# A vision tower on one core: the tail of the token stage in another order, and attentions with the key as the innermost dimension

## The chip, the cores and the metric

The kernel runs on one core of one Trainium2 chip. The metric is the device time of one execution in microseconds; lower is better. The kernel before has a median of 887.18 us over 3 runs (886.36 to 888.2).

## The reference

The input is 128 images x 3 channels x 128 x 128. Everything is float32. Cut to what matters here:

```
h = tok(x)                      # patches -> 9 window tokens + 1 class token per image: (128, 10, 256)
h = h + attn0(layernorm(h))     # 16 heads of 16 channels; scores (token 0, key 9) and (token 9, key 0) masked
h = h + moe(layernorm(h))       # 8 experts, top 2, GELU, layernorm per expert
h = h + attn1(layernorm(h))     # 16 heads; scores clipped to +-10 after scaling, causal
h = h + lora(layernorm(h))
```

An attention is: scores[t, s, head] = sum over 16 channels of q[t]*k[s]; weights = softmax over s; out[t] = sum over s of weights*v[s]; then a projection. The sequence is only 10 tokens long.

## The kernel before

The 128 images lie on the 128 partitions in all that follows the patches, so one tile is one of the 10 tokens, 128 x 256 (`h_at(t)`). The scores of an attention are no matrix product here: DVE (VectorE) or POOL (GpSimd) multiplies 256 channels of a query by 256 channels of n keys (`score_products`, L1121, or L1365 for the products on DVE, which read the query from PSUM), and a sum over 16 channels gives n x 16 scores (`add_up`, L1356). A "row" job is one query with all keys up to its own, a "column" job all earlier queries with one key. POOL's products go to slots in SBUF, two of them in turn; DVE adds them up (`pool_sums`). In attention 0 the columns of tokens 7, 8 and 9 are added up by PE (TensorE) with 16 matmuls each against the identity (`pe_sum_scores`, L1215), and ACT (ScalarE) copies the sums out (L1221).

Stages: (1) the token stage, 9 rounds over 9 patches, PE-bound; its tail (`pe_end`, `act_end`, `pool_end`, `dve_end`) is an order written out by hand for each engine in which the last two window tiles (agg, local and mod of tiles 7 and 8), the class token (`h_at(9)`, L1064) and the first part of attention 0 (turn_x, qk_tile, v_tile and the scores) are interleaved. Engines run their list in order and wait on semaphores. After it there is a barrier of all engines. (2) attention 0: masks, softmax in two halves of 5 tokens (`dve_attention`: L1403 maximum, L1404 subtraction, ACT's exponent L1332, L1408 sum, L1409 reciprocal, L1410 scaling), the value products (`value_products`, L1149: v times weight, the weight repeated over 16 channels) for even tokens on POOL and odd ones on DVE, each into one of two slots of its engine; the sum over keys is made by PE (L1275, 2 x 10 matmuls, 40 in the trace) or, for tokens 1, 3, 5 and 9, by DVE (L1418); PE turns the result (L300), projects it (L294), and `add_o` (L1437) adds it to h and takes statistics (L347, L349), with L354 and L341 (veps, nmr) and POOL's power (L336) at the end of a batch. A projection of token t waits for `add_o` of t-2. (3) the experts, PE-bound, with their weights streamed by DMA on SP's queue; the first weights are asked for when the scores of attention 0 are there. (4) attention 1, the same with n = t+1 keys, where masked scores come from a memset (L1383) and each row of scores is clipped in place (L1353). (5) a low-rank stage.

Scores and weights lie as token, key, head (`a_s`, `a_p`), heads innermost:

```
def score_place(kind, t, n):                                                  # L1143
    s4 = a_s[:, :].rearrange("p (t s h) -> p t s h", t=T, s=T)
    return s4[:, t, 0:n, :] if kind == "row" else s4[:, 0:n, t, :]
```

so the maximum and the sum over keys read with a step of 16 elements, and L1418 with a step of 256. All tensors in these stages are in SBUF but for the PSUM banks that PE writes.

Of the kernel before, what the change touches and what calls it, by code (L numbers as in the profile page):

```python
# [13 lines left out]
ALU = mybir.AluOpType  # L14
# [8 lines left out]
P = 128  # L23
# [40 lines left out]
def vision_tower(nc, d, out):  # L64
    ctx = ExitStack()
    with ctx:
# [861 lines left out]
        def pe_end(pe):  # L928
# [46 lines left out]
        def act_end(act):  # L975
# [109 lines left out]
        VALUES_ON_POOL = (0, 2, 4, 6, 8)  # L1085
        SUMS_ON_DVE = (1, 3, 5, 9)
# [15 lines left out]
        SUMS_ON_PE = {(T - 3, "column"): 0, (T - 2, "column"): 6, (T - 1, "column"): 7}  # L1102
# [12 lines left out]
        def of_query(x, t, n):  # L1115
            return x[:, t * T * H16:(t * T + n) * H16]

        def score_products(eng, kind, t, n, slot):
# [3 lines left out]
                                     a_qkv[:, t, second:second + C].unsqueeze(1).broadcast_to([P, n, C]), ALU.mult)  # L1122

# [30 lines left out]
        def half_scores(x, layer, g):

            nk = HALF if layer == 1 and g == 0 else T
            return x[:, :].rearrange("p (t s h) -> p t s h", t=T, s=T)[:, g * HALF:(g + 1) * HALF, 0:nk, :]


        VALUES_ON_DVE = [t for t in range(T) if t not in VALUES_ON_POOL]  # L1160

        def value_slot(t):
            if t in VALUES_ON_POOL:
                return a_prod[:, 2 + VALUES_ON_POOL.index(t) % 2, :]
            return a_prod[:, VALUES_ON_DVE.index(t) % 2, :]

        def wait_value_slot(eng, layer, t):

            mine = VALUES_ON_POOL if t in VALUES_ON_POOL else VALUES_ON_DVE
            i = mine.index(t)  # L1170
            if i >= 2:
                eng.wait_ge(sem("a_o_turned"), seen(layer, "o_turned", mine[i - 2] + 1))

        def pool_scores(pool, layer, first, last):

            jobs = pool_jobs(layer)
            for i, (t, kind, n) in enumerate(jobs):
                if first <= t < last:
                    pool.wait_ge(sem("a_qkv_made"), seen(layer, "qkv_made", 2 * t + 1))
                    if i >= 2 and summed_on_pe(layer, *jobs[i - 2][:2]):  # L1180
                        pool.wait_ge(sem("a_summed"), list(SUMS_ON_PE).index(jobs[i - 2][:2]) + 1)
                    elif i >= 2:
                        pool.wait_ge(sem("a_pool_prod_used"), used_count(layer, i - 2))
                    score_products(pool, kind, t, n, s_slot[1 + i % 2]).then_inc(sem("a_pool_prod_made"), 1)

        def pool_attention(pool, layer):
            if layer == 0:
                pool_route_constants(pool)
            else:
                inverse_std(pool, *batch_of("attention 1", 0))  # L1190
                inverse_std(pool, *batch_of("attention 1", 1))
                pool_scores(pool, layer, 0, 3)
                inverse_std(pool, *batch_of("attention 1", 2))
                pool_scores(pool, layer, 3, T)
            for t in VALUES_ON_POOL:
                pool.wait_ge(sem("a_p_made"), seen(layer, "p_made", 1 + t // HALF))
                wait_value_slot(pool, layer, t)
# [983 lines left out]
```

## Time and profile before

| | |
|---|---|
| median of 3 runs | 887.18 us |
| the profiled execution | 887.02 us, of which its span is 885.3 us |
| mean granted TensorE clock | 0.917 of full |
| PE, DVE, POOL, ACT busy | 85%, 62%, 45%, 40% of the span |
| tail of the token stage | to 442.4 us |
| attention 0, softmax and values | 442.5 to 512.2 us |
| attention 1, scores to the last projection | 774 to 852.2 us |

A row of the timeline or of the chain of waits begins with its start in microseconds from the span's start and its length. "x2" means that rows were merged. What stands in brackets is how long the engine was idle before it, and what released it. Names: PE matmul, PEld weight load, DVE VectorE, ACT ScalarE, POOL GpSimd. a_s are scores, a_p weights, a_prod value products, w_raw holds the slots of the score products.

### The profile page before, as it was taken

The numbers are of one execution on the slowest core, as the hardware profiler recorded it, in microseconds if no ns is written. First come the engines' busy times: TensorE is split into PE (matmuls) and PEld (weight loads), VectorE is DVE, ScalarE is ACT, GpSimd is POOL, SyncE is SP. The second block draws the span as 40 slices with busy tenths as digits, with TensorE's granted clock in tenths as the row PEclk, the third lists the DMA queues.
The fourth block names the chain that finished last, engine by engine and source line by source line (L and its number), as shares of the span: only waits on it lengthen the run. The fifth ranks groups of instructions, "written<-read, shape, count | busy, mean of one in ns | idle before, by whom it ended". The sixth has DMA issues, their size and how long they took to land.

```text
span 885.3 us, 13257 instructions
## 1 busy us (share of the span) xinstructions
PE 749.5 (85%) x4479; PEld 646.4 (73%) x4479; DVE 548.3 (62%) x1256; ACT 358.4 (40%) x897; POOL 396.1 (45%) x269
## 2 busy tenths in 40 slices
PE   2979999999999999984935964999999999580867
PEld 2869998898988986532835963999999998350756
DVE  1677877787777777667399643222222224799956
ACT  2465665665665655421000141444444443351131
POOL 4555757747757623575254302333333322144310
PEclk9899999999999999985968965999999998695899
DMA  8432132222221110000020038699998860400001
GB/s 269 143 123 80 47 91 77 79 82 83 83 83 42 39 58 1 1 0 0 1 96 1 25 129 324 245 325 325 339 326 332 322 241 19 147 1 0 1 1 60
DMA packets 34490, 102.77 MB, mean 116 GB/s; under 512 B 3624, under 2 KB 12152, under 8 KB 27000
## 3 DMA queue, kind: packets, MB, share of 16 engines
q1 hardware_dynamic: 31832, 94.84, 31.0%
q0 software_dynamic: 2592, 7.10, 2.1%
q8 instruction: 37, 0.61, 0.3%
q14 instruction: 29, 0.24, 0.1%
HBM read 95.75 MB, written 6.17 MB: 115 GB/s over the span
## 4 chain that ended last, share of the span: by engine, by line
PE 72%; DVE 19%; POOL 3%; DMA 2%; issue 1%; ACT 1%; SPq 1%; POOLq 0%; DVEq 0%; ACTq 0%
PE banks L1533 11%; PE banks L1541 11%; PE banks L287 9%; PE banks L289 9%; PE banks L288 9%; PE banks L294 6%; PE banks L1241 5%; PE banks L300 4%; DVE a_o L1418 3%; DVE a_prod L1149 3%; PE banks L1215 2%; DVE a_s L1356 2%; PE banks L1275 2%; PE banks L1871 1%; DVE w_raw L1365 1%
## 5 line engine op out<-in xcount | busy, mean ns | idle before, releaser
L401 POOL TENSOR_TENSOR x_lo<-xraw,x_hi 128x640 fp32r<-128x640 f32 x81 | 129.4, 1605 | 109.8 <-ACT x_hi L395 109.8
L287 PE MATMUL banks<-wc_hi,x_hi 128*128 128x256 f32 x405 | 121.8, 301 | 18.0 <-POOL x_lo L401 12.7
L1631 ACT ACTIVATE hid<-banks,b 128x128 f32<-128x128 f32 x216 | 79.3, 367 | 109.6 <-PE banks L1533 109.5
L288 PE MATMUL banks<-wc_lo,x_hi 128*128 128x256 f32 x405 | 116.4, 287 | 0.0
L289 PE MATMUL banks<-wc_hi,x_lo 128*128 128x256 f32 x405 | 116.4, 287 | 0.0
L287 PEld LDWEIGHTS banks<-wc_hi,x_hi 128*128 128x128 f32 x405 | 79.5, 196 | 20.5 <-issue 12.9
L1790 DVE TENSOR_TENSOR res<-banks,xb 128x256 f32<-128x256 f32 x27 | 11.5, 425 | 126.9 <-PE banks L1541 126.9
L288 PEld LDWEIGHTS banks<-wc_lo,x_hi 128*128 128x128 f32 x405 | 79.6, 196 | 1.8 <-issue 0.2
L289 PEld LDWEIGHTS banks<-wc_hi,x_lo 128*128 128x128 f32 x405 | 79.2, 195 | 0.0
L1275 PE MATMUL banks<-ident,a_prod 128*128 128x128 f32 x372 | 50.6, 301 | 32.7 <-POOL a_prod L1149 32.7
L424 DVE BATCH_NORM_STATS2 stats<-banks 128x6 f32<-128x256 f32 x81 | 34.6, 427 | 69.6 <-ACT pe_sb L418 68.9
L418 ACT ACTIVATE pe_sb<-banks 128x256 f32<-128x256 f32 x81 | 31.0, 383 | 111.8 <-PE banks L289 111.8
L1275 PEld LDWEIGHTS banks<-ident,a_prod 128*128 128x128 f32 x372 | 50.4, 218 | 34.4 <-POOL a_prod L1149 19.5
L287 PE MATMUL banks<-wkv_hi,xg_hi 128*128 128x512 f32 x162 | 70.9, 438 | 4.4 <-DVE xg_lo L485 4.2
L1533 PEld LDWEIGHTS banks<-xT,w_raw 128*128 128x128 f32 x448 | 67.5, 195 | 5.7 <-ACT xT L1619 0.9
L1533 PE MATMUL banks<-xT,w_raw 128*128 128x128 f32 x448 | 69.3, 279 | 0.5 <-ACT xT L1619 0.5
L1241 PE MATMUL banks<-a_w,a_xT 128*128 128x512 f32 (+1 forms) x160 | 65.9, 550 | 1.9 <-DVE w_raw L1365 1.8
L1669 POOL TENSOR_TENSOR y<-bve,mhalf 128x1 f32<-128x1 f32 x27 | 20.4, 755 | 104.6 <-DVE bve L1798 104.6
L1121 POOL TENSOR_TENSOR w_raw<-a_qkv 128x512 f32<-128x512 f32 (+9 forms) x15 | 47.2, 3151 | 44.6 <-ACT a_qkv L1312 20.7
L1541 PE MATMUL banks<-w_raw,hid 128*128 128x256 f32 x224 | 66.9, 380 | 0.0
L336 POOL TENSOR_TENSOR rstd<-veps,mhalf 128x5 f32<-128x5 f32 (+5 forms) x31 | 35.2, 1136 | 67.7 <-DVE veps L354 50.9
L1533 PEld LDWEIGHTS banks<-xT,w1more 128*128 128x128 f32 x416 | 61.8, 191 | 4.7
(293 smaller groups left out, 1830.0 us busy)
## 6 DMA issues: line engine op xcount, KB each, us to landing
w_raw<-in_w SPq DMA_DIRECT2D x28, 1024.0 KB
xraw<-in_x_main SPq DMA_DIRECT2D x27, 768.0 KB
w1more<-in_w SPq DMA_DIRECT2D x13, 1024.0 KB
w2more<-in_w SPq DMA_DIRECT2D x13, 1024.0 KB
xraw<-in_x_rest SPq DMA_DIRECT2D x27, 114.0 KB
yl<-y_rows SPq DMA_DIRECT2D x2, 1028.0 KB, 7.0
a_w<-in_qkv_w SPq DMA_DIRECT2D x2, 768.0 KB, 5.2
x_rows<-w_raw SPq DMA_DIRECT2D x5, 256.0 KB, 2.0
```

The source lines that it names most:

```text
L287: pe.matmul(dst, a[0], b[0], start=start, stop=False)
L288: pe.matmul(dst, a[0], b[1], start=False, stop=False)
L289: return pe.matmul(dst, a[1], b[0], start=False, stop=stop)
L294: last = pe.matmul(dst, aT[:, c * P:(c + 1) * P], w[:, c, a:b], start=(c == 0), stop=(c == CH - 1))
L300: last = pe.transpose(dst[:, c * P:(c + 1) * P], src[:, c * P:(c + 1) * P], ident[:, :])
L401: pool.tensor_tensor(x_lo[:, i % RING_X, :], xraw[:, k].rearrange("p c b -> p (c b)"), x_hi[:, i % RING_X, :], ALU.subtract).then_inc(sem( ...
L1121: return eng.tensor_tensor(slot[:, 0:n * C].rearrange("p (s c) -> p s c", s=n), a_qkv[:, 0:n, first:first + C], a_qkv[:, t, second:second ...
L1241: last = pe.matmul(dst, a_xT[:, t % 2, c * P:(c + 1) * P], a_w[layer][:, c, a:b], start=(layer == 1 and c == 0), stop=(c == CH - 1))
L1275: last = pe.matmul(bank(t % 2, c * P, (c + 1) * P), value_slot(t)[:, k * C + c * P:k * C + (c + 1) * P], ident[:, :], start=(k == 0), stop ...
L1533: last = pe.matmul(bank(fc % 2, 0, P), weights_of(s)[0][:, c * FF + fc * P:c * FF + (fc + 1) * P], xT[:, s % 2, c * P:(c + 1) * P], start= ...
L1541: last = pe.matmul(down_bank(s), hid[:, s % 2, fc, :], weights_of(s)[1][:, fc * C:(fc + 1) * C], start=(fc == 0), stop=(fc == FC - 1))
L1631: act.activation(hid[:, s % 2, fc, :], bank(fc % 2, 0, P), ACT.Gelu, bias=b1[:, bass.ds(e * FC + fc, 1)]).then_inc(sem("gelu_made"), 1)
```

## The change

The tail. On PE, ACT and DVE the steps agg, local and mod of tile 8 come one place earlier; DVE makes the scores of row 5 before it aggregates the class token, and sums column 5 behind that; POOL's power for the class token (`inverse_std` of batch 3) comes before the product of column 6 instead of behind it. POOL's score products get four places (two in `w_raw`, two in `a_prod`), and PE adds up columns 6 and 7 instead of 7, 8 and 9.

The attentions. Scores and weights lie as token, head, key. The maximum is no longer taken in attention 1; there DVE writes sums to PSUM, clips them from there to SBUF, and ACT takes the exponent row by row; the memset of the scores is replaced by one of the weights, on POOL. Half 0 of attention 1's softmax comes before row 9's sum. The reciprocal goes to PSUM. The weights of DVE's own tokens go to PSUM. DVE writes its value products with the key innermost (a step of n elements) and adds them up contiguously, now for all of its tokens. In attention 1 POOL takes tokens 0, 1, 2, 3, 4, 6, 8 and DVE 5, 7, 9.

```diff
 pe_end
+            turn_agg(pe, NW - 1)
             turn_x(pe, 0, 4)
             qk_tile(pe, 0, 3)
-            turn_agg(pe, NW - 1)
+            project_agg(pe, NW - 1)
             v_tile(pe, 0, 3)
-            project_agg(pe, NW - 1)
+            turn_local(pe, NW - 1)
             turn_x(pe, 0, 5)
+            project_mod(pe, NW - 1)
             qk_tile(pe, 0, 4)
-            turn_local(pe, NW - 1)
             v_tile(pe, 0, 4)
             turn_x(pe, 0, 6)
-            project_mod(pe, NW - 1)
...
 pool_end (job numbers now, tokens before)
-            pool_scores(pool, 0, 1, 3)
+            pool_scores(pool, 0, 0, 2)
             inverse_std(pool, *batch_of("attention 0", 1))
+            pool_scores(pool, 0, 2, 3)
+            local_std(pool, NW - 1)
             pool_scores(pool, 0, 3, 4)
-            local_std(pool, NW - 1)
-            pool_scores(pool, 0, 4, 5)
             inverse_std(pool, *batch_of("attention 0", 2))
             value_prod(pool, NW)
             fold_values(pool, NW)
-            pool_scores(pool, 0, 5, 7)
+            pool_scores(pool, 0, 4, 6)
             inverse_std(pool, *batch_of("attention 0", 3))
-            pool_scores(pool, 0, 7, T)
+            pool_scores(pool, 0, 6, T)
 dve_end
+            row_scores(dve, link, 0, 5)
             for half in range(2):
                 aggregate(dve, NW, half)
-            row_scores(dve, link, 0, 5)
+            pool_sums(dve, link, 0, 5)
             dve.wait_ge(sem("proj_done"), NW + 1)
...
             add_eps(dve, "attention 0", 3)
-            pool_sums(dve, link, 0, 5)
-            row_scores(dve, link, 0, 6)
+            shift_of(dve, *batch_of("attention 0", 3))
             pool_sums(dve, link, 0, 6)
-            shift_of(dve, *batch_of("attention 0", 3))
...
-        VALUES_ON_POOL = (0, 2, 4, 6, 8)
-        SUMS_ON_DVE = (1, 3, 5, 9)
+        POOL_VALUES = ((0, 2, 4, 6, 8), (0, 1, 2, 3, 4, 6, 8))
+        DVE_VALUES = tuple([t for t in range(T) if t not in pooled] for pooled in POOL_VALUES)
-        SUMS_ON_PE = {(T - 3, "column"): 0, (T - 2, "column"): 6, (T - 1, "column"): 7}
+        SUMS_ON_PE = {(T - 4, "column"): 0, (T - 3, "column"): 6}
+        def grid(x):
+            return x[:, :].rearrange("p (t h s) -> p t h s", t=T, s=T)
+        def weight_bank(g, a, b):
+            return bank(2 + g, a, b)
+        def scale_bank(g):
+            return bank(4, C + g * HALF * H16, C + (g + 1) * HALF * H16).rearrange("p (t h) -> p t h", t=HALF)
+        def job_place(layer, i):
+            return i % 2 if layer == 1 or i < 4 else (2, 3, 0, 1)[i % 4]
...
+        def row_exponent(act, t):
+            act.wait_ge(sem("a_p_cleared"), 1)
+            act.wait_ge(sem("a_s_made"), seen(1, "s_made", SCORED.index(t) + 1))
+            act.activation(grid(a_p)[:, t, :, 0:t + 1].rearrange("p h s -> p s h"), clipped(t), ACT.Exp, scale=D16 ** -0.5)\
+               .then_inc(sem("a_exp_made"), 1)
...
+                    if t >= 4:
+                        row_exponent(act, SCORED[t - 4])
...
+        SCORED = (0, 2, 1, 4, 3, 6, 5, 8, 7, 9)
         def clip(dve, link, layer, kind, t, n):
             if layer == 1:
-                st = score_place(kind, t, n)
-                link(dve.tensor_scalar(st, st, -40.0, 40.0, ALU.max, ALU.min))
+                dve.tensor_scalar(clipped(t), raw_scores(t, n), -40.0, 40.0, ALU.max, ALU.min)\
+                   .then_inc(sem("a_s_made"), 1)
...
+        def softmax_half(dve, link, layer, g):
...
+            link(dve.tensor_reduce(den_g, p_g, AX, ALU.add))
+            link(dve.reciprocal(scale_bank(g), den_g))
...
+            dve.tensor_tensor(share(p_g, pooled), share(p_g, pooled), scales(pooled), ALU.mult).then_inc(sem("a_p_made"), 1)
+            if mine:
+                dst = weight_bank(g, 0, len(mine) * T * H16).rearrange("p (t h s) -> p t h s", t=len(mine), s=T)
+                link(dve.tensor_tensor(dst, share(p_g, mine), scales(mine), ALU.mult))
...
+            for i, t in enumerate(DVE_VALUES[layer]):
+                n, slot = keys(layer, t), dve_slot(layer, t)
+                by_key = slot[:, 0:n * C].rearrange("p (h d s) -> p s h d", s=n, d=D16)
...
+                link(value_products(dve, layer, t, by_key))
+                dve.tensor_reduce(a_o[:, t * C:(t + 1) * C], slot[:, 0:n * C].rearrange("p (c s) -> p c s", s=n), AX, ALU.add)\
+                   .then_inc(sem("a_o_made"), 1)
                 while added < t - 3:
                     add_o(dve, layer, added)
                     added += 1
```

## Rows read from the trace of the kernel before

**Rows 1.** The page: span, and busy time, share and instructions by engine.
```profile
span 885.3 us, 13257 instructions
PE 749.5 (85%) x4479; PEld 646.4 (73%) x4479; DVE 548.3 (62%) x1256; ACT 358.4 (40%) x897; POOL 396.1 (45%) x269
```

**Rows 2.** The chain of waits, 400 to 442 us: start, length, engine, tile, line.
```profile
402.11 0.44 DVE h L1064
...
404.94 3.43 POOL w_raw L1121
...
410.25 2.57 DVE nmr L341
...
421.06 20.95 PE banks L1215 x96
```

**Rows 3.** The timeline of the same tail.
```profile
393.31 0.76 PE L1239 MATMUL banks<-bias_r,pick 64*128 64x512 f32 x1 [3.65 <-DVE w_raw L1365]
...
408.83 8.47 POOL L1121 TENSOR_TENSOR w_raw<-a_qkv 128x1792 f32<-128x1792 f32 x2
...
412.74 2.27 DVE L1365 TENSOR_TENSOR w_raw<-a_qkv,banks 128x2048 f32<-128x2048 f32 x1
```

**Rows 4.** Groups on DVE, 300 to 560 us: busy us, mean ns; idle before.
```profile
L1418 DVE TENSOR_REDUCE a_o<-a_prod 128x256 f32<-128x2560 f32 x4 | 18.3, 4564 | 0.1
...
L1408 DVE TENSOR_REDUCE a_den<-a_p 128x80 f32<-128x800 f32 x2 | 3.0, 1492 | 0.0
...
L1365 DVE TENSOR_TENSOR w_raw<-a_qkv,banks 128x2560 f32<-128x2560 f32 x1 | 2.8, 2821 | 0.0
L1356 DVE TENSOR_REDUCE a_s<-w_raw 128x160 f32<-128x2560 f32 x1 | 2.8, 2819 | 0.0
...
L1356 DVE TENSOR_REDUCE a_s<-w_raw 128x48 f32<-128x768 f32 x2 | 1.9, 949 | 0.0
```

**Rows 5.** The timeline of attention 0's softmax and values.
```profile
450.86 9.81 POOL L1149 TENSOR_TENSOR a_prod<-a_qkv,a_p 128x2560 f32<-128x2560 f32 x2 [6.77 <-DVE a_p L1410]
...
452.91 3.35 DVE L1410 TENSOR_TENSOR a_p<-a_p,a_rden 128x800 f32<-128x800 f32 x1
...
455.56 7.42 PE L1275 MATMUL banks<-ident,a_prod 128*128 128x128 f32 x40 [13.57 <-POOL a_prod L1149]
456.30 7.06 DVE L1149 TENSOR_TENSOR a_prod<-a_qkv,a_p 128x2560 f32<-128x2560 f32 x1
...
467.84 2.81 DVE L1149 TENSOR_TENSOR a_prod<-a_qkv,a_p 128x2560 f32<-128x2560 f32 x1
...
493.33 2.69 DVE L354 TENSOR_SCALAR veps<-mv 128x4 f32<-128x4 f32 x1
...
498.40 4.63 PE L1275 MATMUL banks<-ident,a_prod 128*128 128x128 f32 x40
...
510.34 1.89 PE L294 MATMUL banks<-a_wo,a_oT 128*128 128x256 f32 x8
```

**Rows 6.** The timeline of attention 1.
```profile
774.31 1.39 DVE L1383 MEMSET a_s<- 128x1600 f32 x1 [0.28 <-ACT a_qkv L1312]
...
781.09 0.60 ACT L1312 ACTIVATE a_qkv<-banks 128x512 f32<-128x512 f32 x1 [0.80 <-PE banks L1241]
...
784.84 3.23 DVE L1353 TENSOR_SCALAR a_s<-a_s 128x80 f32<-128x80 f32 x1
...
794.88 0.60 ACT L1312 ACTIVATE a_qkv<-banks 128x512 f32<-128x512 f32 x1 [1.33 <-PE banks L1241]
...
796.14 1.28 ACT L1332 ACT_TABLE_LOAD   x1
...
819.44 0.69 DVE L1149 TENSOR_TENSOR a_prod<-a_qkv,a_p 128x512 f32<-128x512 f32 x1
...
850.35 1.89 PE L294 MATMUL banks<-a_wo,a_oT 128*128 128x256 f32 x8
```

**Rows 7.** Busy us by engine in tile 0's stretch, PEclk granted clock, DMA share, GB/s.
```profile
455.50:463.00 7.50, 7.42 (x40) 7.26 (x40) 7.47 (x2) 0.00 (x0) 5.17 (x1) 0.62 0.00 0
```

More of the change, by code:

```diff
@@ L1154, in half_scores @@
[L1154 to L1172, printed above, removed]
+            s4 = grid(a_s)
@@ new lines, in score_place, with key_weights @@
+            return (s4[:, t, :, 0:n] if kind == "row" else s4[:, 0:n, :, t]).rearrange(
+                "p h s -> p s h" if kind == "row" else "p s h -> p s h")
+        def key_weights(layer, t, n):
+            if t in DVE_VALUES[layer]:
+                i = [q for q in DVE_VALUES[layer] if q // HALF == t // HALF].index(t)
+                p_t = weight_bank(t // HALF, i * T * H16, (i + 1) * T * H16)
+            else:
+                p_t = a_p[:, t * T * H16:(t + 1) * T * H16]
+            return p_t.rearrange("p (h s) -> p s h", s=T)[:, 0:n, :].unsqueeze(3).broadcast_to([P, n, H16, D16])
@@ new lines, in half_scores, with pool_slot, dve_slot, job_slot @@
+        def half_scores(x, layer, g, first=0, step=1):
+            return grid(x)[:, g * HALF + first:(g + 1) * HALF:step, :, 0:half_keys(layer, g)]
+        def pool_slot(layer, t):
+            return a_prod[:, 2 + POOL_VALUES[layer].index(t) % 2, :]
+        def dve_slot(layer, t):
+            return a_prod[:, DVE_VALUES[layer].index(t) % 2, :]
+        def job_place(layer, i):
+            return i % 2 if layer == 1 or i < 4 else (2, 3, 0, 1)[i % 4]
+        def job_slot(layer, i):
+            k = job_place(layer, i)
+            return s_slot[1 + k] if k < 2 else a_prod[:, k - 2, :]
@@ L1174, in pool_scores @@
         def pool_scores(pool, layer, first, last):
             jobs = pool_jobs(layer)
[L1177 to L1184, printed above, removed]
+            for i in range(first, last):
+                t, kind, n = jobs[i]
+                pool.wait_ge(sem("a_qkv_made"), seen(layer, "qkv_made", 2 * t + 1))
+                earlier_use = [j for j in range(i) if job_place(layer, j) == job_place(layer, i)]
+                if earlier_use:
+                    pool.wait_ge(sem("a_pool_prod_used"), used_count(layer, earlier_use[-1]))
+                score_products(pool, kind, t, n, job_slot(layer, i)).then_inc(sem("a_pool_prod_made"), 1)
@@ L1328, in act_attention @@
                         copy_qkv(act, 1, t - 1)
+                    if t >= 4:
+                        row_exponent(act, SCORED[t - 4])
                 copy_qkv(act, 1, T - 1)
-            for g in range(2):
-                act.wait_ge(sem("a_s_made"), seen(layer, "s_made", g + 1))
-                act.activation(half_scores(a_p, layer, g), half_scores(a_s, layer, g), ACT.Exp, scale=D16 ** -0.5)\
-                   .then_inc(sem("a_exp_made"), 1)
+                for t in SCORED[T - 4:]:
+                    row_exponent(act, t)
+            else:
+                for g in range(2):
+                    act.wait_ge(sem("a_s_made"), g + 1)
+                    act.activation(half_scores(a_p, 0, g), half_scores(a_s, 0, g), ACT.Exp, scale=D16 ** -0.5)\
+                       .then_inc(sem("a_exp_made"), 1)
             for t in range(T):
@@ L1367, in row_scores @@
             dve.wait_ge(sem("a_query_used"), len(rows_on_dve(0)) * layer + rows_on_dve(layer).index(t) + 1)
-            link(add_up(dve, "row", t, n, s_slot[0]))
+            link(add_up(dve, layer, "row", t, n, s_slot[0]))
             clip(dve, link, layer, "row", t, n)
@@ L1395, in half @@
-            def half(x, g):
-                return x[:, g * HALF * H16:(g + 1) * HALF * H16].rearrange("p (t h) -> p t h", t=HALF)
-            def over_s(x, g, nk):
-                return half(x, g).unsqueeze(2).broadcast_to([P, HALF, nk, H16])
-            for g in range(2):
-                s_g = half_scores(a_s, layer, g)
-                link(dve.tensor_reduce(half(a_max, g), s_g.rearrange("p t s h -> p t h s"), AX, ALU.max))
-                dve.tensor_tensor(s_g, s_g, over_s(a_max, g, s_g.shape[2]), ALU.subtract).then_inc(sem("a_s_made"), 1)
@@ L1405, in dve_attention @@
-            for g in range(2):
-                p_g = half_scores(a_p, layer, g)
-                dve.wait_ge(sem("a_exp_made"), seen(layer, "exp_made", g + 1))
-                link(dve.tensor_reduce(half(a_den, g), p_g.rearrange("p t s h -> p t h s"), AX, ALU.add))
-                link(dve.reciprocal(half(a_rden, g), half(a_den, g)))
-                dve.tensor_tensor(p_g, p_g, over_s(a_rden, g, p_g.shape[2]), ALU.mult).then_inc(sem("a_p_made"), 1)
-            dve.wait_ge(sem("a_p_made"), seen(layer, "p_made", 2))
@@ L1412, in dve_attention @@
-            added = 0
-            for t in VALUES_ON_DVE:
-                wait_value_slot(dve, layer, t)
-                ins = value_products(dve, layer, t, value_slot(t))
-                if t in SUMS_ON_DVE:
-                    link(ins)
-                    dve.tensor_reduce(a_o[:, t * C:(t + 1) * C],
-                                      value_slot(t)[:, 0:keys(layer, t) * C].rearrange("p (s c) -> p c s", c=C), AX, ALU.add)\
-                       .then_inc(sem("a_o_made"), 1)
-                else:
-                    ins.then_inc(sem("a_dve_values_made"), 1)
+                link(dve.memset(grid(a_s)[:, 0, :, T - 1], NEG4))
@@ new lines, in dve_attention @@
+                link(dve.memset(grid(a_s)[:, T - 1, :, 0], NEG4))
+                for g in range(2):
+                    s_g = half_scores(a_s, 0, g)
+                    max_g = a_max[:, g * HALF * H16:(g + 1) * HALF * H16].rearrange("p (t h) -> p t h", t=HALF)
+                    link(dve.tensor_reduce(max_g, s_g, AX, ALU.max))
+                    dve.tensor_tensor(s_g, s_g, max_g.unsqueeze(3).broadcast_to([P, HALF, H16, T]), ALU.subtract)\
+                       .then_inc(sem("a_s_made"), 1)
```

84 lines of the change are left out of this document (49 added, 35 removed).

## The prediction

> **What bounds the kernel now.** I read the page first: the span and the busy line [rows 1] show PE at 85% on average, but the slices show two thin places for it, around 390 to 530 us and 750 to 850 us. These are the places that the change touches, so the average says nothing here. Then I read the chain of waits, stage by stage, and the timeline under it.
>
> Stage A, the tail of the token stage (up to 442.5 us). The chain goes through the last tile's residual h(9) at 402.11, two POOL products, a stretched nmr on DVE, the tile's projection and then 21 us of PE adding columns 7, 8 and 9 [rows 2]. The reader is to see that PE works alone at the end, and that the way there is queueing: PE stood 3.65 us for DVE's product of row 5 [rows 3] and then ran tile 8 at about half pace.
>
> Stage B, the softmax and values of attention 0 (442.5 to 512.2), is DVE's: one-source reductions whose inner step is large, and instructions with two SBUF inputs that stand behind POOL [rows 4, 5]. Stage C, attention 1 (774 to 852.2), is DVE's as well [rows 6]. The expert stage between B and C and the LoRA stage behind C are not touched; they start as much earlier as what is before them ends.
>
> **DVE's prices.** A reduction of 768 inner-contiguous elements takes 0.949 us, one of 2560 takes 2.819 [rows 4], so a contiguous one costs 0.15 + 1.04 per 1000 elements. With the key as outer dimension 800 elements took 1.492 and 2560 took 4.564 [rows 4]: 0.67 ns an element more. A product of 2560 with one operand in PSUM takes 2.82 [rows 4], one from SBUF alone 2.81 when POOL is idle [rows 5].
>
> **A.** Removed: column sums 8 and 9 leave PE for DVE; column 6 goes from DVE to PE. Moved: agg(8), local(8) and mod(8) on PE, ACT and DVE; DVE's row 5 ahead of aggregate(9); inverse_std(3) on POOL ahead of column 6; POOL has four slots and no longer waits for PE's sums. No DMA moves.
> 1. h(9). Row 5's product no longer stands behind aggregate(9), so PE's wait of 3.65 goes [rows 3]. PE is then not idle, so tile 8, at half clock from 393.3 to 400, runs partly at full clock; of the 3.4 this can give I take 1.85, since mod(8) may stall PE a little. aggregate(9) ends near 391.5 as before, ahead of PE's arrival. h(9): 402.1 - 5.5 = 396.6; its statistics end 1.3 later, 397.9.
> 2. POOL is idle by then (row 6's product ends at 396), so inverse_std is done at 398.5. But its next instruction, column 6's product, is free to start at once, and nmr (two SBUF inputs) comes 0.1 later. Before, nmr took 2.57 beside a POOL product instead of 0.15, ending with it [rows 2, 3]. I expect the same: nmr ends with column 6's 3.43, at 402.0.
> 3. From 402.0 DVE has, back to back: row 6's sum (1792) 2.0, row 7 two of 2048 4.6, row 8 two of 2304 5.1, column 8's sum 2.3, row 9 two of 2560 5.7, column 9's sum 2.55: 22.3 with gaps 22.5, so 424.5. POOL: columns 7, 8, 9 are ready at 406, 410.5 and 415.6 (8.47 for 1792 + 2048 [rows 3]), before DVE wants each. PE: from nmr's end to its first sum 8.2 us as before (412.8 to 421.1 [rows 2]), 410.2; columns 6 and 7 by the old rate, 20.95/24 = 0.873 per key [rows 2], 13 keys 11.3, 421.5 and a copy, 421.9. DVE ends last. Against 442.4: **-17.9**.
>
> **B**, counted from the first memset. Softmax: four reductions of 800 fall from 1.49 to 0.98 (-2.0). The scaling of half 1 took 3.35 instead of 0.99, until POOL's product ended [rows 5]; now it has one SBUF input: -2.36. Splitting each scaling in two adds 0.15 each, +0.3. So p_made(0) comes at 6.5 instead of 8.3, and DVE is free at 9.9 instead of 13.8. Products: the first took 7.06 for 2.81, behind POOL [rows 5]; now 2.82. Sums 4.56 become 2.82, and tile 7, which PE summed with 40 matmuls, gets one on DVE (+2.82), with PE's 4.63 [rows 5] gone. So 5.7 for each of five tiles: 15.6, 21.3, 27.0, and with two adds (1.05 each: add, statistics, their merge) before each, 34.7 and 43.5; add_eps after tile 3 still stands behind POOL (2.69 for 0.17 [rows 5]), which is in the last number with about 1.
> PE becomes the bound: tile 0 from 11.3 (POOL 4.64) at the low clock, 7.4 [rows 5], 18.7; tile 1 and a projection 20.8; tile 2 25.5; projections with tile 3 and add_o(0) 28.4; tile 4 33.0; projections and tile 5, after add_o(2), 36.1; tile 6 40.8, projection and tile 7 42.2; projection 6 waits for add_o(4) at 43.9, 45.1; tile 8 49.8; the end, as before, 3.2 later: 53.0. Before it was 512.2 - 442.4 = 69.8 [rows 5]. **-16.8**.
> What I price by bounds: the product now writes with a step of 40 bytes. No row has DVE writing so. [...] Above: what a large step costs on reading, +1.71 for 2560 (4.56 against 2.82). [...] POOL reads the weights with the same step: 4.64 to 5.60 (its full-stream product has 2.2 ns an element by the 8.47 above); I take 4.64, since only every 16th element moves on; the upper end costs 1.0, once, at tile 0. Reciprocals that write to PSUM: 0 to 0.1 each.
>
> **C.** The memset of 1.39 goes [rows 6] (POOL's of a_p, about 1.5, falls into 5 us in which POOL waits for the combine). Row 0 moves from 775.7 to 774.05, and PE, which waited for it, with it: a tile's copies come every 2.8, row 9's at 793.2 instead of 794.88 [rows 6]. Clips stood behind POOL (3.23 for 0.2 [rows 6], and 1.59 and 1.09); they now read PSUM. DVE: rows 0, 2, 1 until 778.2, wait for tile 4 780.1, rows 4 and 3 until 784.8, wait 785.6, rows 6, 5 until 791.9, row 8 797.4, row 7 800.0, softmax of half 0 (400 elements: 0.57, 0.65, 0.57) 801.9, row 9 2.82 + 0.3, 805.0, its exponent on ACT 0.5, softmax of half 1 (0.98, 0.65, 0.49, 0.65 and gaps) 808.4. Maxima and subtractions (0.83, 0.58, 1.48, 0.99) are gone, as is the 3.2 of the last scaling. Values start at 808.4, not 819.44 [rows 6]. ACT's exponents, 0.2 to 0.4 each, lie in the 1.0 that ACT idles per tile; the table load of 1.28 [rows 6] now comes at tile 4, where xT is made one tile ahead of its use; without that cover it costs 1.28.
> Values: DVE keeps tiles 5, 7, 9: 3.6, 4.6, 5.7 with two adds between them: 812.0, 818.7, 826.9 (one add waits 1 for PE). PE has tiles 0 to 4 from 802.8, at the low clock at first, and is at tile 6's end by 824.8. Then as before: add 4, projection 6 828.4, tile 8 4.2, 832.6, and 3.0: 835.6 against 852.2 [rows 6]: **-16.6**.
>
> Sum: 887.02 of the profiled execution (its span 885.3 and 1.7 around it) - 17.9 - 16.8 - 16.6 = 835.7. The median is 0.2 above that execution: **836**.
>
> [...] The trace has DVE reductions with a large step 1.6 times as dear as contiguous ones [rows 4]. [...]
> The product with a PSUM operand took 2.82, the one without 2.81 [rows 4, 5]. [...]
>
> **Rivals.**
> 1. Writes with a step cost what reads do. B: 7.35 per tile on DVE, add_o(4) at 51.4, end 60.2, +7.2; C: 0.67 ns on 6144 elements, +3.9. 836 + 11 = 847. For it: one memory. [...] 0.22.
> 2. Slower than before: the same place, but a step on writing costs far more. Rival 1 has 11.1 us for 0.67 ns, 16.6 us per ns; from 3.1 ns an element (a product of 2560 at 10.7 us, 3.8 times itself) the whole 51 is gone, at 4 ns the time is 902. Nothing in the rows has such a factor. 0.02.
> 3. nmr gets in ahead of POOL: A ends 3.4 earlier, 832. For it: in the trace nmr was issued 1.4 after POOL had begun, so the order is untried. Against: POOL's next instruction follows 0.0 us after the last. 0.12.
> 4. PE keeps the low clock through B. It was granted 0.62 in tile 0 with PE full [rows 7], tile 8's 4.63 are full clock [rows 5]. Five tiles at 7.3, ten projections at 1.9 and five turns at 0.6 are 59 from 11.3: 70, B gains nothing, 853. Against: in the stretch where it works without gaps it got the high clock. 0.05.
> 5. The weights in PSUM do not free DVE: a product still stands behind POOL's. Then the first two or three of B wait 2 to 4 each, C's 2: +10, 846. Against: the product of 2048 with the query in PSUM took 2.27, its own price, beside POOL's products [rows 3]. 0.05. That the edits do nothing of what they say has 0.01.
> The forecast itself, 831 to 841, has 0.53.
>
> **How the numbers follow.** The range takes in the forecast, rival 3 and rivals 1 and 5 with a few us for my step-by-step errors in A (h(9) between 395 and 402 moves the end by 5): 829 to 850. Within 0.2% (1.8 us, about what a measurement can tell from no change) I put 0.01, slower 0.02, faster 0.97.
>
> **What would show it.** A: the h(9) addition near 397, nmr stretched to some 3.4, PE's sums over before DVE's last sum near 424. B: DVE products of 2560 at 2.8, sums at 2.8, none behind POOL; PE busy from 11 us on and waiting only for add_o. C: clips at 0.2 throughout, values from 808 less what A and B gave. Wrong if products take 4.5, if PE's clock stays low, or if h(9) does not move.

## The result and the profile after

850.86 us (median of 4 runs, 849.11 to 853.41) against 887.32 before: ratio 0.9592, 95% interval 0.9559 to 0.9624. The forecast was 836, the range 829 to 850: the sign was right, 51 us were promised and 36.5 came. The profiled execution took 849.13; by stages, from the two traces:

| us | before | after | change | forecast |
|---|---|---|---|---|
| A, to the first memset of the softmax | 442.46 | 423.83 | -18.6 | -17.9 |
| B, to the end of the last projection | 69.8 | 64.0 | -5.8 | -16.8 |
| experts, to their first addition to h | 234.1 | 234.3 | +0.1 | 0 |
| C, from there to the end of the last projection | 105.9 | 93.1 | -12.8 | -16.6 |
| what is left | 33.1 | 32.2 | -0.8 | 0 |

The page of the kernel after, as [rows 1] of before:

```profile
span 847.4 us, 13115 instructions
...
PE 729.8 (86%) x4399; PEld 630.6 (74%) x4399; DVE 535.9 (63%) x1253; ACT 358.6 (42%) x904; POOL 396.5 (47%) x272
```

Stage A in its timeline, which answers [rows 2, 3]. The reader is to see h(9) at 395.9, nmr stretched to 3.37 behind POOL, PE's sums over before DVE's last sum, and DVE ending the stage: each as forecast. The whole stage shifts a little from one execution to another: in the ten traces of this document in which the tail has these instructions (experiments 1, 2, 4 to 9 and 11, and this one) h(9) starts between 394.0 and 396.4, and the first memset follows it by 27.9 to 28.0 in every one.

```profile
395.88 0.42 DVE L1065 TENSOR_TENSOR h<-banks,rows 128x256 f32<-128x256 f32 x1 [2.33 <-PE banks L294]
...
397.83 3.37 DVE L341 SCALAR_TENSOR_TENSOR nmr<-mv,rstd 128x1 f32<-128x1 f32 x1 [0.66 <-POOL rstd L336]
...
408.38 11.56 PE L1234 MATMUL banks<-w_raw,ident 128*128 128x96 f32 x64
...
421.02 2.55 DVE L1393 TENSOR_REDUCE a_s<-a_prod 128x144 f32<-128x2304 f32 x1
...
423.83 0.07 DVE L1452 MEMSET a_s<- 128x16 f32 x1 [0.26 <-DVEq L282]
```

Stage B, the groups of DVE's value products and sums (busy us, mean ns of one), against [rows 4]. The sum fell from 4.564 to 2.821, the product rose from 2.81 to 4.731:

```profile
L1158 DVE TENSOR_TENSOR a_prod<-a_qkv,banks 128x2560 f32<-128x2560 f32 x5 | 23.7, 4731 | 0.0
L1469 DVE TENSOR_REDUCE a_o<-a_prod 128x256 f32<-128x2560 f32 x5 | 14.1, 2821 | 0.2
```

and its timeline, against [rows 5]. No product stands behind POOL any more, but PE twice waits long for an addition to h that DVE makes behind a tile (6.91 and 4.55), and after each of these waits its 40 matmuls take 5.9 instead of 4.63 (granted clock 0.76 and 0.78):

```profile
456.67 2.04 PE L294 MATMUL banks<-a_wo,a_oT 128*128 128x256 f32 x4 [6.91 <-DVE h L1485]
...
458.51 5.95 PE L1290 MATMUL banks<-ident,a_prod 128*128 128x128 f32 x40
...
477.34 2.04 PE L294 MATMUL banks<-a_wo,a_oT 128*128 128x256 f32 x4 [4.55 <-DVE h L1485]
...
479.18 5.87 PE L1290 MATMUL banks<-ident,a_prod 128*128 128x128 f32 x40
...
485.96 1.89 PE L294 MATMUL banks<-a_wo,a_oT 128*128 128x256 f32 x8
```

Two stretches of the same trace, tile 2 and then tile 4 behind the first wait (last but two: the granted clock, 1.00 and 0.76):

```profile
442.00:447.00 5.00, 4.74 (x39) 4.40 (x38) 4.97 (x2) 0.66 (x2) 4.25 (x1) 1.00 0.01 3
...
458.50:464.40 5.90, 5.90 (x42) 5.89 (x41) 5.87 (x2) 0.00 (x0) 0.00 (x0) 0.76 0.00 0
```

Stage C, against [rows 6]: the table load in front of row 4's product, the first value product (1536 elements in 2.96, a contiguous one would be 1.75), a wait of PE for an addition, and 28 matmuls slowed behind it (granted clock 0.65 in 798.7 to 803.6; the same 28 took 3.29 in experiment 10):

```profile
753.46 1.28 ACT L1335 ACT_TABLE_LOAD   x1
...
756.32 1.49 DVE L1402 TENSOR_TENSOR w_raw<-a_qkv,banks 128x1280 f32<-128x1280 f32 x1 [2.41 <-ACT a_qkv L1327]
...
784.45 2.96 DVE L1158 TENSOR_TENSOR a_prod<-a_qkv,banks 128x1536 f32<-128x1536 f32 x1
...
791.11 3.85 DVE L1158 TENSOR_TENSOR a_prod<-a_qkv,banks 128x2048 f32<-128x2048 f32 x1
...
797.76 1.10 PE L294 MATMUL banks<-a_wo,a_oT 128*128 128x256 f32 x4 [3.67 <-DVE h L1485]
...
798.70 4.92 PE L1290 MATMUL banks<-ident,a_prod 128*128 128x128 f32 x28
...
813.27 1.89 PE L294 MATMUL banks<-a_wo,a_oT 128*128 128x256 f32 x8
```

### The profile page after: what moved, and what is told of

Same layout as the page of the kernel before. It is cut to its first block, busy times and chain, and to the rows that moved or that the text cites. A ratio compares the mean times of both kernels' runs of the same rounds, so it can differ in the third digit from the quotient of the medians.

```text
span 847.4 us, 13115 instructions
## 1 busy us (share of the span) xinstructions
PE 729.8 (86%) x4399; PEld 630.6 (74%) x4399; DVE 535.9 (63%) x1253; ACT 358.6 (42%) x904; POOL 396.5 (47%) x272
## 4 chain that ended last, share of the span: by engine, by line
PE 69%; DVE 20%; POOL 3%; DMA 2%; issue 2%; ACT 1%; SPq 1%; POOLq 1%; DVEq 0%; ACTq 0%
PE banks L1581 12%; PE banks L1589 11%; PE banks L287 10%; PE banks L289 10%; PE banks L288 10%; PE banks L294 6%; PE banks L300 4%; DVE a_prod L1158 4%; PE banks L1260 4%; DVE a_o L1469 2%; DVE a_s L1393 2%; DVE banks L1393 1%; DVE w_raw L1402 1%; PE banks L1290 1%; PE banks L1919 1%
## 5 line engine op out<-in xcount | busy, mean ns | idle before, releaser
L287 PE MATMUL banks<-wc_hi,x_hi 128*128 128x256 f32 x405 | 121.9, 301 | 17.9 <-POOL x_lo L401 12.6
L1290 PE MATMUL banks<-ident,a_prod 128*128 128x128 f32 x324 | 46.5, 311 | 24.4 <-POOL a_prod L1158 24.4
L336 POOL TENSOR_TENSOR rstd<-veps,mhalf 128x5 f32<-128x5 f32 (+5 forms) x31 | 32.6, 1053 | 73.7 <-DVE veps L354 57.0
L1290 PEld LDWEIGHTS banks<-ident,a_prod 128*128 128x128 f32 x324 | 46.2, 227 | 25.9 <-issue 15.6
L289 PE MATMUL banks<-wkv_hi,xg_lo 128*128 128x512 f32 x162 | 64.5, 398 | 0.0
L288 PE MATMUL banks<-wkv_lo,xg_hi 128*128 128x512 f32 x162 | 63.9, 395 | 0.0
```

The lines of the kernel that those rows point to most:

```text
L287: pe.matmul(dst, a[0], b[0], start=start, stop=False)
L288: pe.matmul(dst, a[0], b[1], start=False, stop=False)
L289: return pe.matmul(dst, a[1], b[0], start=False, stop=stop)
L1290: last = pe.matmul(bank(t % 2, c * P, (c + 1) * P), slot[:, k * C + c * P:k * C + (c + 1) * P], ident[:, :], start=(k == 0), stop=(k == ns ...
```

## Experiments

Two things were open: what makes the product 4.73 (its output's step, or its weights in PSUM, read with a step too), and where B lost 3.8 more than the rival with that price had said (60.2). Each experiment is the changed kernel with the edit shown or described, in 4 runs against 7 of the kernel before (887.0 to 887.1), unless said otherwise.

**1. The write without its step.** The sums still read as in the changed kernel and so add the wrong elements: only the times count.

```diff
-                by_key = slot[:, 0:n * C].rearrange("p (h d s) -> p s h d", s=n, d=D16)
+                by_key = slot[:, 0:n * C].rearrange("p (s h d) -> p s h d", s=n, d=D16)
```

> The changed kernel with one view altered: DVE's value products are written contiguously (key, head, channel) while its sums still read groups of neighbouring elements, so for DVE's tiles the sums add the wrong elements. All durations that do not depend on the output's step stay. Theory W (the 40-byte step of the product's output costs): products of 2560 fall from 4.72 to 2.82, the sums stay 2.82, PE becomes the bound of attention 0's values, B falls from 64.0 to 53-56, C by another 3-4: 836 to 840. Rival P (the weights in PSUM, read with a step of 40 bytes between heads, make the 4.72): products stay at 4.7 and the time at 850 to 851. Rival H (both halves of it): products near 3.7, 843 to 846.

Measured: 833.74 us, ratio 0.9406 (0.9389 to 0.9424). Groups of B and its last projection:

```profile
L1469 DVE TENSOR_REDUCE a_o<-a_prod 128x256 f32<-128x2560 f32 x5 | 14.1, 2820 | 0.2
L1158 DVE TENSOR_TENSOR a_prod<-a_qkv,banks 128x2560 f32<-128x2560 f32 x5 | 14.0, 2806 | 0.0
...
474.60 1.89 PE L294 MATMUL banks<-a_wo,a_oT 128*128 128x256 f32 x8
```

The weights are read as before, and the product is back at 2.81: the step of the output is the whole cost. B is 53.6 (from a first memset at 422.90; forecast 53.0), C 17.6 under the kernel before (forecast 16.6). So the forecast, 836, was a right sum within 2.3 us for a kernel in which this write is free.

**2. The step back on the reading side**: the edit of 1, and `"p (c s) -> p c s"` of the sum (L1469) back to `"p (s c) -> p c s"`.

> The changed kernel with DVE's value products written contiguously and its sums reading with the key outermost, as before the change; it computes the whole result. Theory W: product 2.82 and sum 4.56 make 7.4 for a tile against 7.54 now, so the step has only moved from the sum to the product: 848.5 to 851. Rival P: product 4.72 and sum 4.56, 1.74 more for each of 5 tiles in attention 0 and 3.9 in attention 1: 860 to 864.

Measured: 850.93 us, 0.9596 (0.9578 to 0.9614), the changed kernel's time. In B:

```profile
L1469 DVE TENSOR_REDUCE a_o<-a_prod 128x256 f32<-128x2560 f32 x5 | 22.8, 4550 | 0.2
L1158 DVE TENSOR_TENSOR a_prod<-a_qkv,banks 128x2560 f32<-128x2560 f32 x5 | 14.0, 2805 | 0.0
```

2.81 + 4.55 against 4.73 + 2.82: turning the products around only moved the step from the instruction that reads to the one that writes. What B and C gained comes from the rest of the change.

**3 and 4. Each part alone.** 3: the attentions of the change on the old tail (old order, columns 7, 8, 9 on PE, two slots); 4: the kernel before with the new tail.

> Only the attentions' part of the change, on the old tail of the token stage (old order, PE summing columns 7, 8 and 9 from two slots). If the parts add: 850.9 + 18.6 = 869.5 (869 to 871), the tail ending near 442.4. Rival: the tail's new slots or order had also cost the attention something (the first values find other engines busy), then 866 to 868.

> Only the tail's part of the change, with the attentions as before: the tail ends at 423.8 to 424.5 and the time is 887.3 - 18.6 = 868.7 (868 to 869.5) if the parts add. Rival: a part of the tail's gain comes back in the old softmax, since POOL's column products or the copies of PE's sums now lie beside it: 870 to 872.

Measured: 867.46 (0.9781, 0.9756 to 0.9807) and 867.19 (0.9781, 0.9765 to 0.9797), 2.0 and 1.5 us faster than expected. 3 thus lies in the range of its rival, that the new tail costs the attention something. Its trace does not settle this: B is 62.7 there (64.0 in the changed kernel), but C is 95.2 (93.1). The end of A in 3, then in 4:

```profile
441.84 0.07 DVE L1455 MEMSET a_s<- 128x16 f32 x1 [14.35 <-ACTq L282]
```
```profile
422.73 0.07 DVE L1398 MEMSET a_s<- 128x16 f32 x1 [0.25 <-DVEq L282]
```

The spans of the profiled executions, 866.7 and 865.3 against 885.3, give 18.6 and 20.0, together 38.6 where the whole change has 37.9; the medians give 39.5 (both against 887.07) and 36.5. The parts add within 0.7 in the one and 3 in the other; the four times of the changed kernel lie in two pairs (849.1 and 852.6 to 853.4), which leaves that much open.

**5. The values stored turned**, so that nothing on DVE or POOL has a step.

```diff
-            act.activation(a_qkv[:, t, 2 * C:3 * C], bank(5), ACT.Copy).then_inc(sem("a_qkv_made"), 1)
+            act.activation(a_vT[:, :, t], bank(5), ACT.Copy).then_inc(sem("a_qkv_made"), 1)
...
-                        last = pe.matmul(bank(t % 2, c * P, (c + 1) * P), slot[:, k * C + c * P:k * C + (c + 1) * P],
+                        last = pe.matmul(bank(t % 2, c * P, (c + 1) * P), by_channel[:, c * P:(c + 1) * P, k],
```

> The changed kernel with the values of each tile stored turned, [channel][key], by ACT's copy out of PSUM (256 elements, its write takes the 40-byte step), so that DVE and POOL read values, weights and write products all without a step, and PE's 128x128 loads of POOL's products have the step of 40 bytes instead. It computes the whole result. Theory (the step costs DVE, wherever DVE has it; it costs little on ACT's 256 elements): DVE's product 2.82 and sum 2.82, ACT's copy 0.4 to 0.6 instead of 0.38, 833 to 837, like the run with the contiguous writing. Rival 1: PE's loads with a step are slow, 128x128 from 0.115 to 0.2 us each, 40 of them for each tile +3.4, then 845 or more. Rival 2: POOL's product of 4.7 changes, since its weights are no longer read with a step but each 16th time; if it falls PE's first tile starts up to 0.5 earlier, if it rises over 5 the slots come late.

Measured: 855.5 us, 0.9643 (0.9614 to 0.9672), 4.6 slower than the changed kernel. One tile's matmuls, and groups of B (and of ACT's copies):

```profile
446.55 9.14 PE L1292 MATMUL banks<-ident,a_prod 128*128 128x128 f32 x40
...
L1292 PE MATMUL banks<-ident,a_prod 128*128 128x128 f32 x200 | 45.9, 393 | 16.0 <-POOL a_prod L1159 16.0
...
L1159 POOL TENSOR_TENSOR a_prod<-a_vT,a_p 128x2560 f32<-128x2560 f32 x5 | 26.3, 5266 | 20.4 <-PE banks L1292 15.3 <-DVE a_p L1437 5.0
...
L1159 DVE TENSOR_TENSOR a_prod<-a_vT,banks 128x2560 f32<-128x2560 f32 x5 | 14.0, 2807 | 0.0
L1331 ACT ACTIVATE a_vT<-banks 128x256 f32<-128x256 f32 x10 | 6.4, 640 | 6.8 <-PE banks L1261 6.8
```

DVE was served as the theory had it, and everyone else paid: PE's 200 matmuls with a 40-byte step in what they load took 45.9 us against 28.4 (a tile's 40, at a granted clock of 1.00 in both, 9.14 against 4.63), POOL's product 5.27 against 4.75, ACT's copy 0.64 against 0.385. Rival 1 held, with 4.5 us a tile where it had put 3.4, and rival 2 with it: POOL's product rose over 5.

**6. Pairs**: the product in two instructions that write with a step of 8 bytes.

```diff
+                by_pair = slot[:, 0:n * C].rearrange("p (k h d j) -> p k h d j", j=2, h=H16, d=D16)
-                link(value_products(dve, layer, t, by_key))
+                for j in range(2):
+                    made = dve.tensor_tensor(by_pair[:, :, :, :, j],
+                                             a_qkv[:, j:n:2, 2 * C:3 * C].rearrange("p s (h d) -> p s h d", d=D16),
+                                             key_weights(layer, t, n)[:, j:n:2], ALU.mult)
+                link(made)
...
+                dve.tensor_reduce(a_o[:, t * C:(t + 1) * C], slot[:, 0:n * C].rearrange("p (k c j) -> p c k j", c=C, j=2), mybir.AxisListType.XY, ALU.add)
```

> The changed kernel with DVE's products written in pairs of keys: two instructions for a tile (even and odd keys), each writing with a step of 8 bytes, and sums that read pairs of neighbours, the pairs 1 KB apart. It computes the whole result. [...] Rival S2 (every step other than one element costs the same): product 4.9, sum 3.7 to 4.6: 8.6 to 9.5, 856 to 863. Rival S3 (a step of 8 bytes is free on both sides): product 2.95, sum 2.9, 834 to 838.

Measured: 834.75 us, 0.9404 (0.9372 to 0.9435): S3, to which I had given no reason. Groups of B:

```profile
L1469 DVE TENSOR_TENSOR a_prod<-a_qkv,banks 128x1280 f32<-128x1280 f32 x10 | 14.4, 1478 | 0.0
L1473 DVE TENSOR_REDUCE a_o<-a_prod 128x256 f32<-128x2560 f32 x5 | 14.1, 2820 | 0.2
```

A step of 8 bytes costs nothing on writing (1.48 is 0.15 + 1.04 x 1.28, the price of a contiguous one), and neither does reading pairs that lie 2 KB apart (2.820 for the sum, 2.821 when contiguous). B is 53.9: this is the forecast's kernel, with the whole result computed.

**7. The additions to h one tile earlier.**

```diff
-                while added < t - 3:
+                while added < t - 2:
```

> The changed kernel with one condition altered: DVE adds the projections to the residual up to tile t - 3 instead of t - 4 after the sum of tile t (add_o(0) after tile 3's sum). Theory: of attention 0's 64.0 us about 4 beyond the dear products come from PE standing for add_o(0) and add_o(4), 6.9 and 4.5, and working at the low clock afterwards; with the adds earlier PE has tile 8 done before DVE's last sum, and only the turn and projection of tile 9 are left behind it: the last addition at about 483 instead of 489, attention 1 by 1 to 3 too: 842 to 846. Rival: DVE's work alone bounds the stage, an earlier add only waits for PE's projection and delays the next product by the same: 850 to 852.

Measured: 841.62 us, 0.9486 (0.9457 to 0.9515), 9.2 under the changed kernel. PE in B:

```profile
455.82 2.04 PE L294 MATMUL banks<-a_wo,a_oT 128*128 128x256 f32 x4 [2.77 <-DVE h L1485]
...
465.31 1.10 PE L294 MATMUL banks<-a_wo,a_oT 128*128 128x256 f32 x4 [1.22 <-DVE h L1485]
...
467.46 4.63 PE L1290 MATMUL banks<-ident,a_prod 128*128 128x128 f32 x40
...
476.80 3.28 PE L294 MATMUL banks<-a_wo,a_oT 128*128 128x256 f32 x8
```

The wait of 6.91 is 2.77, tile 8's matmuls take 4.63 and are over when DVE's last sum begins, and only tile 9's turn and projection are left behind it. B is 58.2 with the dear products still in it, 5.8 shorter, and C 3.4 shorter. In this execution A ended 1.9 earlier and the experts took 1.4 longer (235.7), neither of which the edit touches.

**8. The weights of DVE's tokens left in SBUF** (`weight_bank(...)` replaced by DVE's part of `a_p`, in place).

> The changed kernel with DVE's weights scaled in SBUF like POOL's, not written to PSUM; the output keeps its step. Theory L (two SBUF inputs beside POOL's product wait for it, PSUM weights avoid that): in attention 0 the first product stands behind POOL's two, about 4 longer, others 0 to 4 each where POOL is at work: 855 to 862. Rival N (a product with 4.7 us of strided writing does not compete with POOL): 850 to 852. In either case a product not beside POOL shows whether the step costs as much with both operands in SBUF: 4.7.

Measured: 855.25 us, 0.9634 (0.9601 to 0.9667), theory L at its lower end. Groups of B, DVE's first product beside POOL's, and one with POOL idle:

```profile
L1158 POOL TENSOR_TENSOR a_prod<-a_qkv,a_p 128x2560 f32<-128x2560 f32 x5 | 36.7, 7361 | 11.3 <-PE banks L1290 6.3 <-DVE a_p L1435 5.0
L1158 DVE TENSOR_TENSOR a_prod<-a_qkv,a_p 128x2560 f32<-128x2560 f32 x5 | 28.2, 5642 | 0.0
...
434.01 6.17 DVE L1158 TENSOR_TENSOR a_prod<-a_qkv,a_p 128x2560 f32<-128x2560 f32 x1
...
463.08 4.71 DVE L1158 TENSOR_TENSOR a_prod<-a_qkv,a_p 128x2560 f32<-128x2560 f32 x1
```

4.71 alone, with both operands in SBUF: the step's price again does not hang on PSUM. The weights in PSUM save the conflict with POOL, worth 4.4 us of time, and it falls on both engines: DVE's first three products took 6.2 to 6.4, POOL's first four 31.9 together, 8.0 each, and its fifth, which began with DVE at a sum, 4.75.

**9. Which steps pay** (one run; the kernel leaves keys out and sums part of the elements, so only the lengths count).

> A measuring kernel, not a faster one: in attention 0 DVE's products of tiles 1, 3, 5 and 7 are split into 3, 4, 5 and 2 instructions, which write with steps of 12, 16, 20 and 8 bytes (768, 512, 512 and 1280 elements each; tiles 1 and 3 leave one and two keys out), tile 9 keeps 40; the sums of tiles 7 and 9 read every second and every fourth element (8 and 16 bytes). Only the lengths of these instructions count. A contiguous one is 0.15 + 1.04 per 1000 elements: 0.95, 0.68, 0.68, 1.48. [...] Rival TB (it pays by the step in proportion until the 0.70 ns of 24 to 40 bytes): 12 bytes near 1.1, 16 bytes 0.85. Rival T8 (only steps over some limit between 16 and 24 bytes pay): 0.95 and 0.68 up to 16 bytes. Reads: the sums with 8 and 16 bytes, 1280 and 640 elements, 1.48 and 0.82 if free, 2.4 and 1.25 at the price of the 1 KB step.

Measured, DVE's groups in B (busy us, mean ns of one): 12 bytes (768 elements), 16 and 20 bytes together (512), 8 bytes (1280), then the sums that read with 8 bytes (L1477) and with 16 (L1481):

```profile
L1471 DVE TENSOR_TENSOR a_prod<-a_qkv,banks 128x512 f32<-128x512 f32 x9 | 8.7, 1098 | 0.0
...
L1471 DVE TENSOR_TENSOR a_prod<-a_qkv,banks 128x768 f32<-128x768 f32 x3 | 3.3, 1175 | 0.0
...
L1471 DVE TENSOR_TENSOR a_prod<-a_qkv,banks 128x1280 f32<-128x1280 f32 x2 | 2.9, 1466 | 0.0
...
L1481 DVE TENSOR_REDUCE a_o<-a_prod 128x128 f32<-128x640 f32 x2 | 2.5, 1268 | 0.0
L1477 DVE TENSOR_REDUCE a_o<-a_prod 128x256 f32<-128x1280 f32 x1 | 1.5, 1486 | 0.0
```

The contiguous price was read from the lengths of single instructions, so the mean of one is what compares with it; busy time divided by the count is up to 0.13 less, because neighbours overlap. An instruction at 12 bytes takes 1.18 (0.95 if free), at 16 bytes 1.09 and at 20 bytes 1.10 (0.68): per element 0.3 ns and 0.8 ns more. The products of attention 1 in the changed kernel give 0.8 at 24 bytes (2.96 for 1.75, 1536 elements) and at 32 (3.85 for 2.28, 2048), and that of attention 0 0.75 at 40 bytes (4.73 less 2.81, over 2560). At 8 bytes nothing: writing 1.47, reading 1.49. Reading with 16 bytes, 1.27 against 0.82, is 0.7 ns. So TB was near at 12 bytes (1.1, measured 1.18) and too low at 16 (0.85, measured 1.09); T8's free 16 bytes (0.68) are refuted. The price begins between 8 and 12 bytes and all of it is there at 16; no run shows why it does. (Tile 9's product was written without a step here, and took 2.81.)

**10. POOL lets nmr go first.**

```diff
+            pool.wait_ge(sem("nmr_made"), batch_of("attention 0", 3)[0] + 1)
             pool_scores(pool, 0, 6, T)
```

> The changed kernel with one wait more on POOL: its product of column 6 waits until DVE has written nmr of the last batch of attention 0. Theory (nmr stands behind POOL's product for 3.2 of its 3.37 us and everything behind it with it): nmr takes 0.15, the tail ends near 420.7 instead of 423.8, 847 to 848.5. Rival: POOL's products, 0.4 later, become what DVE waits for in the end (column 9 needed at 417.7, there by 415.5 to 416) or PE's chain from h(9) sets the end anyway: 850 to 851.

Measured: 847.89 us, 0.9562 (0.9537 to 0.9587): 3.0 less. nmr, the end of A, and, from C, the product over tile 8's keys, which took 4.18 in the changed kernel's trace:

```profile
397.75 0.16 DVE L341 SCALAR_TENSOR_TENSOR nmr<-mv,rstd 128x1 f32<-128x1 f32 x1 [0.66 <-POOL rstd L336]
...
420.86 0.07 DVE L1453 MEMSET a_s<- 128x16 f32 x1 [0.26 <-DVEq L282]
...
805.39 6.00 PE L1291 MATMUL banks<-ident,a_prod 128*128 128x128 f32 x36
```

From h(9) to the first memset it is 25.1 here and in experiment 12, and 27.9 to 28.0 in the ten traces without the edit: 2.9 of the 3.4 that the rival on nmr had as its price. In this execution C was 2.9 longer than in the changed kernel's, with a wait of 4.15 in front of these matmuls instead of 2.52. The two pairs of times of the changed kernel may be the same thing, now slow and now not, or the shifts of stage A, which reach 2.4; only one of the four was traced, so this stays open. The 3.0 between the medians is 1.2 against the lower pair and some 5 against the upper one, so the price rests on the traces and not on the medians.

**11 and 12. What beats both.** 11 is 6 and 7 together; 12 adds 10 and an exponent of two elements on ACT ahead of attention 1.

> Pairs (steps of 8 bytes, 834.75) and the additions to the residual one tile earlier (841.62 alone, 9.2 less than the changed kernel). In the run with pairs PE bounds attention 0's values and still stands 1.33, 0.97 and 2.33 for additions, and runs tile 8 at the low clock (5.75 instead of 4.63). Theory: these 5.7 go partly, 828 to 832. Rival: with DVE's tiles at 5.7 the additions come in time as they are, and an earlier place only makes DVE wait for PE: 834 to 836.

> Pairs, additions earlier, POOL's wait for nmr, and ACT's table of exponents loaded ahead of attention 1 by an exponent of two elements, in the 15 us that ACT is idle there, instead of at tile 4 (where it delayed row 4's product by 2.4). If all add: the time of the run before in this call - 3 (nmr) - 0.5 to 2 (table): 824 to 828. Rival: the table load was covered after all, since PE and not DVE set attention 1's pace: only nmr's 3 come off.

Measured: 825.39 us (0.9306, 0.928 to 0.9333) and 825.13 us (0.9303, 0.9276 to 0.9329). In 11 B is 47.1, from 423.87 to the end of

```profile
469.03 1.92 PE L294 MATMUL banks<-a_wo,a_oT 128*128 128x256 f32 x8
```

and C 85.0. The two gains, 16 from the pairs and 9 from the additions, add up: 25.5. That is below the 828 to 832 expected: the 5.7 of waiting and low clock that the pairs had left in B were all that the theory counted, and against experiment 6 B gave 6.8 and C, which it had not counted, another 4.0. In 12 B ends 2.5 earlier again, but the time is the same, which neither the theory (the 3 of nmr and 0.5 to 2 more come off) nor its rival (the 3 alone) had. First, the ten us in which the experts' first products start, in 11 and then in 12 (last but two: the granted clock):

```profile
504.00:514.00 10.00, 8.93 (x51) 8.28 (x52) 0.42 (x1) 3.60 (x10) 1.17 (x2) 0.75 0.39 125
```
```profile
502.50:512.50 10.00, 9.48 (x46) 8.73 (x47) 0.43 (x1) 3.37 (x10) 0.89 (x1) 0.64 0.30 113
```

PE was granted 0.64 of full clock there where it had 0.75, and the expert stage took 236.1 instead of 234.5: 1.7 of the 2.5 were given back, and another 0.7 behind C (33.5 for 32.8). It need not be so: in experiment 10 A ended as much earlier and the experts took 234.2. Each is one trace, and what decides it was not looked into. Second, the table load in 12:

```profile
704.17 1.28 ACT L1341 ACT_TABLE_LOAD   x1
...
738.11 1.49 DVE L1404 TENSOR_TENSOR w_raw<-a_qkv,banks 128x1280 f32<-128x1280 f32 x1 [1.79 <-ACT a_qkv L1328]
```

It left row 4's way, whose wait fell from 2.41 in experiment 11 to 1.79 only, and row 6's wait rose from 0.17 to 0.79. C kept its length (84.9 for 85.0): the load had been covered, as the rival said.

## Why the prediction was right in sign and wrong in size

**A was right**: -18.6 against -17.9, in mechanism too (h(9) 395.9 for 396.6, nmr stretched and ending at 401.2 for 402.0, first memset 423.8 for 424.5; only PE's first sum, 408.4 for 410.2, was off by more than 1, and nothing waited for it). That it came within 0.7 is partly luck, since h(9) moves by 2.4 between executions.

**The step that failed** is the one priced by bounds, DVE's product that "now writes with a step of 40 bytes": 2.82, or 1.71 more. I took 2.82, the price of a contiguous write; that the step costs nothing on writing was my estimate, from no row, and no run shows it for 40 bytes. Measured is 4.73, 1.9 above the value taken and 0.2 above the upper end (4.53); with the write made contiguous it is 2.81 and the time 833.74 (experiment 1), so this one term took 17.1 us. The forecast was missed by 14.9, since the rest of the sum had erred by 2.3 the other way. The nearest row was the same data read with a large step at 1.6 times the price, and that should have been the value: experiment 2, with the step moved to the reading side, has 1.73 more for the sum (4.55), where writing has 1.92 more for the product.

**What fell with it in B.** "PE becomes the bound" needed DVE's 5.7 for a tile; at 7.55 DVE stayed it. Experiment 1 gives 53.6 for the forecast's 53.0, so the other terms (softmax with p_made at 6.5, DVE free at 9.9, no product behind POOL, tile 7 on DVE) were right.

**The rival with that price was 3.8 short in B** (60.2 against 64.0). It had add_o(4) at 51.4 (52.95 measured) and 8.8 behind it (11.1 measured). The slower DVE brings the additions late, PE idles 6.9 and 4.6 for them, and the 40 matmuls after each wait take 5.9 instead of 4.63; experiment 7 took 5.8 out of B by moving them alone.

**C**: mis-sized by 3.8. That this is the rival's own 3.9 for the writes is partly luck: against experiment 1 (-17.6) the writes cost 4.8, and the rest of C was 1.0 better than the forecast's -16.6. (0.67 ns on 6144 elements is 4.1 besides, not 3.9.) The table load was covered, as put (C is 84.9 with the load ahead of attention 1 in experiment 12, 85.0 without in 11).

**Rivals.** Nmr ahead of POOL: did not happen; its price (3.4) measures 2.9 in experiment 10. PE at the low clock all through B: it was low in tile 0 (0.58 in 434 to 442) and behind the waits (0.76 and 0.78), but 1.00 in tile 2. A product's operand in PSUM cost nothing, as in the sum: 2.806 with one (experiment 1), 2.81 without [rows 5]. Weights in PSUM that don't free DVE: refuted by the trace (all five at 4.7) and by experiment 8, in which leaving them in SBUF costs 4.4, where the rival had 10 for the conflict. The range ended at 850, where rival 1 stood at 847 with a chance of 0.22: it had no room for what rival 1 would bring with it. With the waits that the slower DVE causes on PE, 3.8, rival 1 stands at 851, and its own spread reaches above that.

## What to carry to other kernels

When a layout is turned so that a reduction reads without a step, look who has the step now: the writer pays what the reader paid (1.92 us more for 2560 elements against 1.73), and on PE's loads the same step doubled the time (9.14 for 4.63). A middle layout can free both: in fp32 two neighbours for each place (a step of 8 bytes) cost neither side anything (1.48 for 1280 elements written, 2.82 for 2560 read) and were worth 16 us here. Where one engine both computes tiles and makes a small operation that releases another engine, place that small operation by the time at which it is needed: one condition was worth 9 us.

## What the runs showed of the hardware that was not expected

- DVE pays for a step in SBUF on writing as on reading, by bytes: 8 free, 12 bytes 0.3 ns an element, 16, 20, 24, 32 and 40 bytes 0.75 to 0.8 (writing); 8 free, 16 bytes 0.7, 1 KB 0.68 (reading; the last is 4.55 in experiment 2 against 2.82).
- PE's 128x128 fp32 products with a step of 40 bytes in the loaded operand: 9.14 us for 40 against 4.63, both at a granted clock of 1.00.
- A product on DVE with two SBUF inputs beside one of POOL slowed both (6.2 to 6.4 for 4.71, 8.0 for 4.75), where before the change DVE stood until POOL had ended [rows 5]. Which of the two happens was not looked into; the slowed products of DVE write with a step and read their weights with one, those of before did neither.
- 2.5 us gained ahead of the experts came back as 1.7 us of a longer expert stage in experiment 12 (granted clock at its start 0.64, in experiment 11 0.75), and not in experiment 10.
